# A two-pass adjacency kernel: another interleaving of its first pass, another order of its norms, and four of eight kept chunks

## The reference

```python
e   = x + par * (diag * x @ W)                 # W_u for the first 2048 rows, W_i for the rest
h   = adj @ (adj.T @ e)                        # two products with the 105 MB matrix
x1  = layernorm(2 * x + layernorm(h) * gamma + beta)
deg = adj.sum(axis=0) + 1
z   = rsqrt(deg) * (x1 @ W1)
out = layernorm(x1 + relu(rsqrt(deg) * (adj.T @ z + z) + b))
```

## Time and profile before

| | |
|---|---|
| median of 3 runs | 639.91 us (639.69 to 640.78) |
| the profiled execution, its own time | 641.78 us |
| its span, first to last instruction | 640.1 us |
| TensorE busy | 600.1 us, 94% of the span |
| VectorE busy | 334.5 us, 52% |
| ScalarE, GpSimd busy | 138.8 us, 108.4 us |
| moved by DMA | 204.8 MB, mean 320 GB/s |

### The profile page before, as it was taken

One profiled execution on the slowest core, in us unless ns is written; L12 is line 12 of the kernel. 1 busy time (PEld: TensorE's weight loads), 2 busy tenths in 40 slices (PEclk: granted clock), 3 DMA queues, 4 the chain that ended last, 5 costly groups with the idle time before them and its releaser, 6 DMA issues.

```text
span 640.1 us, 10729 instructions
## 1 busy us (share of the span) xinstructions
PE 600.1 (94%) x4785; PEld 235.2 (37%) x4785; DVE 334.5 (52%) x355; ACT 138.8 (22%) x208; POOL 108.4 (17%) x126
## 2 busy tenths in 40 slices
PE   6989999999999999999999999999999999978775
PEld 5433333333333333333333335554343434313112
DVE  3789467768767776876675782644140402103004
ACT  2015060421506042150605117311000101001001
POOL 3006051240705122050503104100000000000000
PEclk9989999999999999999999999999999999999998
DMA  7998299959778694977879497699999999999991
GB/s 256 387 377 291 98 363 377 388 189 351 269 268 298 240 387 163 372 266 259 290 256 387 150 387 266 244 349 338 383 409 410 410 411 409 412 409 410 412 396 63
DMA packets 86002, 204.82 MB, mean 320 GB/s; under 512 B 4539, under 2 KB 7099, under 8 KB 85957
## 3 DMA queue, kind: packets, MB, share of 16 engines
q1 hardware_dynamic: 84196, 202.77, 85.1%
q10 hardware_dynamic: 1760, 1.38, 0.6%
HBM read 202.82 MB, written 1.31 MB: 319 GB/s over the span
## 4 chain that ended last, share of the span: by engine, by line
PE 76%; DMA 14%; DVE 7%; POOL 1%; ACT 1%; issue 1%; SPq 0%; ACTq 0%; DVEq 0%; POOLq 0%
PE psum L751 28%; PE psum L861 21%; PE psum L954 12%; DMA slot<-in_adj_dram 9%; PE psum L869 6%; DMA last_slot<-in_adj_dram 4%; DVE slot L583 3%; PE psum L795 2%; PE psum L745 2%; PE psum L974 1%; POOL turned L354 1%; DVE turn L562 1%; PE psum L722 1%; PE psum L934 1%; PE psum L922 1%; DVE last_slot L583 1%
## 5 line engine op out<-in xcount | busy, mean ns | idle before, releaser
L583 DVE STREAM_TRANSPOSE slot<-slot 128x2048 f32<-128x2048 f32 x80 | 177.7, 2279 | 75.9 <-PE psum L751 75.9
L751 PE MATMUL psum<-slot,E 128*64 128x512 f32 x768 | 173.8, 603 | 3.0 <-DVE slot L589 2.6
L861 PE MATMUL psum<-slot,T 32*64 32x512 f32 x2560 | 142.5, 590 | 0.0
L354 POOL COPY turned<-last_slot 32x1024 f32<-32x1024 f32 x80 | 84.4, 1055 | 285.8 <-DVE last_slot L583 281.5
L954 PE MATMUL psum<-slot,E 128*64 128x512 f32 x512 | 115.0, 596 | 10.5 <-DMA slot<-in_adj_dram 9.7
L751 PEld LDWEIGHTS psum<-slot,E 128*64 128x64 f32 x768 | 53.2, 138 | 114.4 <-issue 113.4
L404 ACT ACTIVATE turned<-last_slot 32x1024 f32<-32x1024 f32 x80 | 84.3, 1054 | 40.6 <-DVE last_slot L583 38.9
L861 PEld LDWEIGHTS psum<-slot,T 32*64 32x64 f32 x2560 | 55.9, 132 | 84.4 <-issue 84.4
L694 DVE TENSOR_TENSOR T<-psum,dinv 128x256 f32<-128x256 f32 x10 | 4.2, 425 | 144.1 <-PE psum L974 143.7
L395 ACT ACTIVATE T<-T 32x256 f32<-32x256 f32 x60 | 24.8, 414 | 224.1 <-DVE T L567 222.9
L954 PEld LDWEIGHTS psum<-slot,E 128*64 128x64 f32 x512 | 35.2, 137 | 86.5 <-issue 60.0
(11 more groups left out here) (110 smaller groups left out, 268.4 us busy)
## 6 DMA issues: line engine op xcount, KB each, us to landing
slot<-in_adj_dram SPq DMA_DIRECT2D x152, 1024.0 KB, 14.3
last_slot<-in_adj_dram SPq DMA_DIRECT2D x30, 1024.0 KB, 7.7
turned<-in_adj_dram SPq DMA_DIRECT2D x10, 1024.0 KB, 15.1
X<-in_x_dram SPq DMA_DIRECT2D x5, 256.0 KB, 5.1
out_dram<-T ACTq DMA_DIRECT2D x10, 128.0 KB, 5.8
T<-in_L_gnn_W_u_dram ACTq DMA_DIRECT2D x2, 16.0 KB, 2.9
T<-in_L_gnn_W_i_dram ACTq DMA_DIRECT2D x2, 16.0 KB, 4.6
beta_b<-in_L_gnn_ln_beta_dram SPq DMA_DIRECT2D x1, 32.0 KB, 11.5
```

The source lines that it names most:

```text
L354: nc.gpsimd.tensor_copy(turned[c * Q32:(c + 1) * Q32, a].rearrange("p h k j r -> p (h k j) r"), last_blocks[a * Q32:(a + 1) * Q32, :, c, : ...
L583: v.transpose(parts, parts).then_inc(chunk_cut, 1)
L751: return mm(acc[half[b % 2], :], E[:, b, :], view[:, b % CB, :], start=(b < 2), stop=(b >= NB - 2))
L861: last = mm(acc[half[h], a, :], T[step % 2][rows_a, jb, (c - a) % 4, :], slot[step % 2][rows_a, h:NF:2, :, cols], start=False, stop=False, ...
```

## The change

- `h_step`: in the middle steps the order is group 0, five chunks of t, groups 1 and 2, five chunks of t, group 3 (which sets `slots_used`), `turn_t`, `h_last`. Steps 0 and 9 keep their order.
- The five matmuls that zeroed the accumulators are gone; the first product of each bank is issued with `start=True`.
- VectorE's order in the steps: in step 0 `copy_tT` and `copy_t` stand ahead of the cuts of chunks 7, 8 and 9; in the later steps the cut of chunk 8 stands between `copy_tT` and `copy_t`.
- At the beginning `turn_x(0)` and `turn_x(1)` stand ahead of the scales' transposes, and the mean of each weight matrix is taken as that matrix lands.
- Four chunks of strip 1 are kept and restored; (1,4) to (1,7) are loaded again, after `h_done` 1 and, in SP's order, ahead of (0,9) and (1,9). `FIRST` has another order at its head.
- The norms: one ScalarE copy takes h groups 2 and 3; groups 1 to 4 are squared from that copy; `norm_h(1)` stands behind `make_group(0)`; the last products 2 and 3, and with them `h_done` 2, stand behind the first four sweeps.

```diff
-FIRST = [(0, 0), (0, 1), (0, 2), (0, 3), (1, 0), (1, 1), (1, 2), (1, 3), (0, 4), (0, 5), (1, 4), (1, 5),
+FIRST = [(0, 0), (0, 1), (1, 0), (1, 1), (0, 2), (0, 3), (1, 2), (1, 3), (0, 4), (0, 5), (1, 4), (1, 5),
          (0, 6), (0, 7), (1, 6), (1, 7), (0, 8), (1, 8), (0, 9), (1, 9)]
-FIRST_LOADS = [(s, q) for s, q in FIRST if s == 0 or q >= NF]
+KEPT = 4
+FIRST_LOADS = [(0, q) for q in range(NF)] + [(0, 8), (1, 8)] + [(1, q) for q in range(KEPT, NF)] + [(0, 9), (1, 9)]
...
-                if q < NF:
+                if q < NF and s == 0:
                     sp.wait_ge(slots_used, NJ - 1)
+                elif q < NF:
+                    sp.wait_ge(h_done, 1)
...
             square_h(0)
             copy_hT(0)
             copy_hT(1)
             root_h(0)
+            copy_hT(2, 2)
             square_h(1)
-            for g in (2, 3):
-                copy_hT(g)
-                square_h(g)
-            root_h(1)
             copy_yT(0)
             root_y(0)
+            root_h(1)
+            square_h(2)
...
             for step in range(NJ):
-                for q in range(NF):
+                early = NF - 1 if step == 0 else NF
+                for q in range(early):
                     cut_chunk(step * NQ + q)
                 copy_tT(step)
+                if step > 0:
+                    cut_chunk(step * NQ + early)
                 copy_t(step, step % 2)
-                for q in range(NF, NQ):
+                for q in range(early if step == 0 else early + 1, NQ):
                     cut_chunk(step * NQ + q)
...
             restore(0)
             norm_h(0)
-            norm_h(1)
             restore(1)
             make_group(0)
+            norm_h(1)
             restore(2)
             make_group(1)
             norm_h(2)
             restore(3)
             make_group(2)
             norm_h(3)
-            restore(4)
             norm_h(4)
             make_group(3)
-            restore(5)
-            restore(6)
             make_group(4)
-            restore(7)
...
-            pe.wait_ge(xT_ready, NG)
-            for i in range(5):
-                last = mm(bank[i], zeros[:, 0:P], zeros, start=True, stop=True)
-            last.then_inc(banks_zeroed, 1)
...
-                each = JB // T_ROUNDS
-                for n in range(T_ROUNDS):
-                    if step == 0:
-                        t_pairs(step + 1, n * HS // T_ROUNDS, (n + 1) * HS // T_ROUNDS)
...
+                between_t = 0 < step < NJ - 1
+                if step == 0:
+                    t_pairs(1, 0, HS // 2)
...
+                h_group(step, 0)
+                if final:
+                    turn_degrees()
+                if between_t:
+                    t_pairs(step + 1, 0, HS // 2)
+                h_group(step, 1)
+                if step == 0:
+                    t_pairs(1, HS // 2, HS)
+                h_group(step, 2)
+                if between_t:
+                    t_pairs(step + 1, HS // 2, HS)
+                h_group(step, 3).then_inc(slots_used if not final else h_done, 1)
...
-            last_products(range(0, 2))
+            last_products([0])
             sum_h(0)
             turn_h(0)
             turn_h(1)
-            sum_h(1)
             turn_y(0)
-            last_products(range(2, JB)).then_inc(h_done, 1)
+            last_products([1])
             sum_y(0)
             project_y(0)
+            sum_h(1)
+            first_round(1)
             turn_y(1)
-            first_round(2)
+            first_round(1)
             sum_y(1)
             project_y(1)
+            first_round(2)
+            last_products([2, 3]).then_inc(h_done, 1)
             turn_h(2)
             sum_h(2)
             first_round(2)
```

More of the change, by code:

```diff
@@ L20 @@
 NF = 8
-T_ROUNDS = 2
 ACT_MOVES = [(a, c) for a in range(4) for c in range(4) if (a + c) % 2]
@@ L85, in build @@
         hT = [turn[0][:, :], turn[1][:, :], between[:, 0:JW], between[:, JW:2 * JW], turn[0][:, :]]
-        hh = [after[:, 0:JW], after[:, JW:2 * JW], between[:, 2 * JW:3 * JW], between[:, 3 * JW:4 * JW], after[:, 0:JW]]
+        hh = [after[:, 0:JW], after[:, 0:JW], between[:, 2 * JW:3 * JW], between[:, 3 * JW:4 * JW], after[:, 0:JW]]
         yy = after[:, JW:2 * JW]
@@ L141, in build @@
         residual_centred = sem("residual_centred")
-        banks_zeroed = sem("banks_zeroed")
         slot_loaded = [[sem(f"slot_loaded{i}_{q}") for q in range(NF)] for i in range(2)]
@@ L203, in build, with h_sums, copies @@
         finish_chain = sem("finish_chain")
+        def h_sums(g, n):
+            if g < NG - 1:
+                return acc[:, :, g * P:(g + n) * P].rearrange("p a (k r) -> p a k r", r=Q32)
+            return bank[4].rearrange("p (a k r) -> p a k r", k=CB, r=Q32)
+        def copies(g):
+            return g + 1 if g < 3 else g
         def feat(v, n=GB):
@@ L412, in _, with copy_hT @@
             nc.scalar.activation(dinv[:, :], dinv[:, :], ACT.Sqrt).then_inc(dinv_root, 1)
[L414 to L420, removed]
+            def copy_hT(g, n=1):
                 act.wait_ge(h_done, 1 if g < NG - 1 else 2)
@@ L423, in copy_hT @@
                     act.wait_ge(h_turned, 1)
-                nc.scalar.activation(hT[g].rearrange("p (k a r) -> p a k r", k=CB, r=Q32), h_sums(g),
+                to = hT[g] if n == 1 else between[:, 0:n * JW]
+                nc.scalar.activation(to.rearrange("p (k a r) -> p a k r", a=4, r=Q32), h_sums(g, n),
                                      ACT.Copy).then_inc(hT_ready, 1)
             def square_h(g):
[L428 to L432, removed]
+                if g == 0:
+                    act.wait_ge(h_done, 1)
+                    nc.scalar.activation(hh[g].rearrange("p (k a r) -> p a k r", k=CB, r=Q32), h_sums(g, 1),
+                                         ACT.Square).then_inc(hh_ready, 1)
+                else:
+                    act.wait_ge(hT_ready, copies(g))
+                    if g in (1, NG - 1):
+                        act.wait_ge(h_summed, 1 if g == 1 else 2)
+                    nc.scalar.activation(hh[g], hT[g], ACT.Square).then_inc(hh_ready, 1)
             def root_h(g):
@@ L444, in copy_yT @@
                     act.wait_ge(y_summed, g)
-                else:
-                    act.wait_ge(h_summed, 2)
                 nc.scalar.activation(yy, y_turn, ACT.Square).then_inc(yy_ready, 1)
@@ L472, in _ @@
             root_h(2)
-            copy_hT(4)
-            square_h(4)
+            square_h(3)
             copy_yT(2)
@@ L477, in _ @@
             root_h(3)
+            copy_hT(4)
+            square_h(4)
             copy_yT(3)
@@ L526, in _ @@
             v = nc.vector
[L528 to L531, removed]
             for i in range(2):
+                dve.wait_ge(weights_loaded[i], 16 * 2)
+                link(v.tensor_reduce(mean_w[:, i:i + 1], WM[:, 2 * i, :], AX, ALU.add))
+                link(v.tensor_scalar(mean_w[:, i:i + 1], mean_w[:, i:i + 1], -1.0 / F, None, ALU.mult))
                 for h in half:
@@ L765, in _ @@
             pe.wait_ge(ident_ready, 1)
+            turn_x(0)
+            turn_x(1)
             pe.wait_ge(scales_loaded, 16 * 4)
@@ L769, in _ @@
             last.then_inc(diagT_done, 1)
-            turn_x(0)
-            turn_x(1)
             project_x(0)
@@ L781, in _ @@
             project_x(4)
-            for q in range(1, NQ - 1):
+            for q in range(1, NQ):
                 first_sums(q)
-            pe.wait_ge(xT_ready, NG)
-            for i in range(5):
-                last = mm(bank[i], zeros[:, 0:P], zeros, start=True, stop=True)
-            last.then_inc(banks_zeroed, 1)
-            first_sums(NQ - 1)
             pe.wait_ge(fold_ready, 3)
@@ L809, in turn_h @@
             def turn_h(g):
-                pe.wait_ge(hT_ready, g + 1)
+                pe.wait_ge(hT_ready, copies(g))
                 if g == 0:
@@ L862, in h_group @@
                                       slot[step % 2][rows_a, h:NF:2, :, cols],
-                                      start=False, stop=False, skip_group_check=True)
+                                      start=step == 0 and jb == 0 and c == 0, stop=False, skip_group_check=True)
                 return last
@@ L869, in h_last @@
                     last = mm(bank[4][half[h], :], T[step % 2][:, jb, 0, :], turned[:, :, h, :, jb, :],
-                              start=False, stop=False, skip_group_check=True)
+                              start=step == 0 and jb == 0, stop=False, skip_group_check=True)
                 return last
@@ L876, in h_step @@
                 final = step == NJ - 1
-                each = JB // T_ROUNDS
-                for n in range(T_ROUNDS):
-                    if step == 0:
-                        t_pairs(step + 1, n * HS // T_ROUNDS, (n + 1) * HS // T_ROUNDS)
[L881 to L893, removed]
+                between_t = 0 < step < NJ - 1
+                if step == 0:
+                    t_pairs(1, 0, HS // 2)
```

(9 more changed lines are left out.)

## The result

The changed kernel takes 660.67 us (660.18 to 662.22 in four runs) where the kernel before takes 640.0, now the median of four runs: a ratio of 1.0323, with a 95% interval of 1.0306 to 1.034. Its profiled execution took 661.06 us with a span of 659.3, which is 19.2 us more than before.

The account below looks back on a forecast made before the run. TensorE was taken to bound the kernel until the strips end, the stream of loads after. Slower strips, a late h_done 2 and four more loads put the last landing 15.1 us later, giving 655.0 us, range 646 to 661.

Parts of the forecast that it names:

- What bounds it: Whole kernel: TensorE bounds it until the strips are done at 395.5 us, the stream of loads after that.
- part 1: Middle steps: slots_used to slots_used, through the fifth chunk's landing, takes 38.2 us where it was 37.05.
- The order in a strip: Steps 1 to 8: copy's 0.74 us hidden, fifth chunk 1.9 us late; turn_t of step 9 starts 9.2 us later.
- The page's fit of a transfer: Slot bursts: the fit lands the fifth chunk at 14.0 us, in time for 15.2; forecast followed measured 16.3 to 18 rows instead.
- The cut of chunk 8: VectorE in later steps: cutting ahead of copy_t costs nothing behind group 3; without that group some 1.2 us a step.
- The start: Up to 78.9 us: zeroing, transposes, weight means and copy order gain 0, with 1 us as the other end.
- Between the passes: After the strips: h_done 2 moves from 8.3 to 20.5 us after h_done 1; the stream then runs full, 205.0 us.
- Two gates close together: Between the passes: last of 14 loads lands at 425.1, h_done 2 comes at 425.2; stream stands still 2.8 us.
- The sum: Whole kernel: last landing 638.4 instead of 623.3, 15.1 us later; span 655.2, time 655.0 us.
- The loads in time: Rival, strips: fifth chunk within 15.0 us, only the hidden copy left, strip 36.3, time 639.8 us; chance 0.09.
- The four loads in slack: Rival, between the passes: strips slower, but four extra loads fall into slack, end 8.3 us later, 648.2 us; chance 0.12.

Follow-up runs that it names:

- three chunks: Changed kernel with group 0, three chunks of t, group 1, two chunks, group 2, five chunks, group 3: 646.39 us, 1.008.
- two groups first: Kernel before with groups 0 and 1, five chunks of t, group 2, five chunks, group 3 in middle steps: 638.12 us, 0.9944.
- the three runs: Changed kernel with h_done 2 ahead of all sweeps: 658.22 us, 1.0274; with eight chunks kept: 659.21 us, 1.0303; with both: 652.87 us, 1.0191.
- good strips: Changed kernel, steps reordered: groups 0, 1, five chunks, group 2 and half of group 3, five chunks, other half: 642.36 us, 1.0024.
- half a group: Kernel before, steps reordered: groups 0, 1, five chunks, group 2 and half of group 3, five chunks, other half: 634.98 us, 0.9914.

## Why the prediction was right, and where it was off

The forecast was 655.0 us in a range of 646 to 661. The measured 660.67 lies 0.3 us inside the upper end, and two of the four executions (661.06 and 662.22) lie above it. The direction and the mechanism were found by the working; that the median still falls into the range is in part luck.

**What bounds it: right for the kernel before.** TensorE up to h_done 1, the stream after. In the strips of the changed kernel it is the round from slots_used over the fifth landing back to slots_used, as part 1 said.

**The order in a strip: right in mechanism and sign, low in size.** The copy's 0.74 us vanished, the wait for the fifth chunk took its place, and moving that chunk's demand (the runs with three chunks or two groups first) takes the wait away. The strip was put at 38.2 us and measured 38.86; eight times 0.66 is 5.3 us, nearly the whole miss. Most of it is the landing: the fifth comes 17.37 us after the first issue in the mean, where I had 16.9, 0.5 us of the 0.66. I had left out the second burst of before (17.7) and taken the mean of the other seven; the last section shows that those seven were of two kinds. The fifth issues of two bursts of the changed kernel (xcount, KB, us to landing), issued at 198.32 in the burst of 195.24 and at 354.72 in that of 351.96, land 17.5 and 16.3 us after the first issue:

```profile
slot<-in_adj_dram SPq DMA_DIRECT2D x1, 1024.0 KB, 14.4
...
slot<-in_adj_dram SPq DMA_DIRECT2D x1, 1024.0 KB, 13.5
```

The rest is a thing that I could have read before: the eight matmuls of a chunk take 1.75 us inside a row of forty, but 1.94 to 1.96 behind a wait, so the fifth sum takes 0.2 us more than I had. The 0.2 us that I had for the issue are there too, but ahead of it: group 3, at whose end SP waits, takes 3.70 us for 3.53, and the issue follows 0.02 later.

**The page's fit of a transfer**, 2 us and the bytes at 436 GB/s (the Trainium skill, DMA: Bandwidth & Descriptors, Anatomy of one DMA; measured there on the GpSimd path), gives the fifth landing 14.0 us after the first issue, an estimate, and would have had it in time. The changed kernel's waits and its landings (16.3 to 18.1) disagree with it for a burst of 1 MiB loads from SP, as the rows of before did.

**The cut of chunk 8: right in sign**, a cost only without group 3. I had named 1.2 us a step; measured alone it is half of that, 0.6, since h_last hides the rest.

**The start: right.** The burst behind step 0 is issued at 78.89, where it was 79.03 with the old order. Over all runs it comes between 78.0 and 79.5 with the old start and between 77.6 and 81.7 with the new one: no gain of the start's edits shows.

**Between the passes: right.** h_done 2 came 20.8 us after h_done 1 (20.5 forecast), and from its release to the last sweep it took 211.8 us, where 2.7 + 5.4 + 205.0 = 213.1 were forecast. Two gates close together were forecast: the last of the fourteen loads lands at 431.80, 1.1 us behind the release by h_done 2, and the three runs found both.

**The sum.** The span rose by 19.2 us, not 15.1: 5.1 more in the strips, 0.3 more up to h_done 2, 1.3 less in the stream. The medians differ by 20.7. The profiled execution of before lay 1.8 us over its median of 640.0, that of the changed kernel only 0.4 over its own; I had taken the same distance for both, and this is another 1.4 us of the miss.

**The rivals fell.** The loads in time: no, the chain waits for them in each of the eight strips. The four loads in slack: no; the changed kernel with good strips still loses its 7 us, and with h_done 2 early the eight kept chunks gain 5 us (1.0274 to 1.0191).

## What to carry to other kernels

When work is moved forward in a loop to hide a short wait, ask of each thing it reads when its buffer was released and how long the whole queue of loads behind that release takes; the distance from release to first use (here 21.2 us, cut to 8.2) is a resource like a buffer. Cover a short wait with as little work as does it: half a group hid the same copy and left the loads their time. And where several waits stand in one in-order queue of loads, taking away one of two gates shows next to nothing, which doesn't prove that it was harmless.

## What was not expected of the hardware

The bursts of 1 MiB loads are not even: in the changed kernel the fifth landing came 16.3 to 18.1 us after the first issue with the same eight loads each time, and shortening the moves beside them changed the mean by 0.2 us only. The traces show what stands beside the late ones. The page lists a queue of its own of the kind "instruction" (transfers, MB, share of 16 engines):

```profile
q8 instruction: 37, 0.61, 0.4%
```

These are transfers of 16 KB, each on one of the 16 DMA engines and some 1.1 us long. In a burst each chunk lands 2.7 us behind the one before, but the chunk in flight beside such a transfer mostly comes 3.2 to 4.3 us behind (a few delays of 0.4 to 0.6 us have none beside them). In the burst of 234.20 the transfer starts at 242.71, and the first three chunks land 5.8, 8.5 and 12.7 us after the first issue. In the kernel before, four of the eight bursts have one between the first issue and the fifth landing (17.1 to 17.8 us), and four have none (16.3 to 16.7). In the changed kernel six have one (17.3 to 18.1), and two have none (16.8 and 16.3). Where a burst of before has none, it comes behind the fifth landing, where TensorE doesn't wait: 17.4 to 19.3 us after the first issue. So the 16.9 that I took was a mean of two kinds of bursts, and after the change the late kind is the common one. No run moved or removed such a transfer; that it delays the chunk is read from the times and not shown by an experiment.
